# Self-attention of a decoder block: identity cast first, parts stored singly, the maxima's transfers issued by GpSimd, warming matmuls between maxima

## The reference

```python
x = x + _L0_attn_ref(_layernorm(x), Wq, Wk, Wv, Wo)
# in it, with 16 heads of 8 features (dk = 8):
q, k, v = proj(Wq), proj(Wk), proj(Wv)          # [4, 16, 512, 8]
q, k = rotary(q), rotary(k)
scores = q @ k.T / sqrt(8)                       # 512 x 512 for each of 64 heads
out = softmax(scores) @ v
return merge_heads(out) @ Wo.T
```

## Time and profile before

| | us |
|---|---|
| median of 3 executions | 2113.87 |
| fastest, slowest | 2107.86, 2125.06 |
| profiled execution, its own time | 2109.2 |
| its span | 2107.4 |
| first maximum matmul starts | 66.10 |
| first exp starts | 103.65 |
| last exp starts and ends | up to 276.4 |
| output block ends, cross-attention starts | about 308 |

### The profile page before, as it was taken

The page is one execution under the profiler, slowest core; times in us unless marked ns, Lnnn a source line. Parts: engine busy times, 40 slices in busy tenths (PEclk is TensorE's granted clock), DMA queues, the critical chain, the costliest instruction groups (busy, mean ns, idle before and its releaser), DMA issues.

```text
span 2107.4 us, 46811 instructions
## 1 busy us (share of the span) xinstructions
PE 1964.4 (93%) x19020; PEld 1159.9 (55%) x19020; DVE 1525.9 (72%) x1744; ACT 1311.2 (62%) x1857; POOL 995.1 (47%) x722
## 2 busy tenths in 40 slices
PE   6499887779999999999999999999999999999996
PEld 3122133356666666666666666666666666666663
DVE  4599526477877778777877787777877787778762
ACT  3077764456666667666766676666766676667662
POOL 7000004165656555555555565555555565556540
PEclk9599998899999999999999999999999999999998
DMA  4320000044334344333443344533444333343330
GB/s 112 75 54 11 2 32 5 26 121 112 96 101 108 104 127 121 101 99 101 126 113 99 99 111 121 131 93 92 119 121 121 99 89 102 101 117 104 98 104 23
DMA packets 102453, 194.55 MB, mean 92 GB/s; under 512 B 12480, under 2 KB 32448, under 8 KB 102112
## 3 DMA queue, kind: packets, MB, share of 16 engines
q1 hardware_dynamic: 102240, 191.56, 34.6%
HBM read 123.77 MB, written 54.66 MB: 85 GB/s over the span
## 4 chain that ended last, share of the span: by engine, by line
PE 76%; ACT 2%; issue 1%; POOL 1%; DVE 0%; DMA 0%; SPq 0%; ACTq 0%; POOLq 0%
PE ps L1297 16%; PE ps L1372 9%; PE ps L1327 8%; PE ps L1349 8%; PE ps L1382 8%; PE ps L1306 8%; PE ps L1401 6%; PE ps L1360 4%; PE ps L1337 4%; PE ps L1411 3%; PE ps L1322 2%; ACT l_v_tok L1463 1%; PE ps L1389 1%; POOL l_rot L1270 0%; POOL l_rot L1273 0%
## 5 line engine op out<-in xcount | busy, mean ns | idle before, releaser
L1270 POOL TENSOR_TENSOR l_rot<-l_rot,l_rot_s 128x1024 f32<-128x1024 f32 x192 | 455.3, 2371 | 1.0 <-DVE l_rot_s L1614 1.0
L1259 POOL COPY l_kb<-l_kb 128x512 f32<-128x512 f32 x95 | 63.1, 664 | 683.7 <-ACT l_kb L1497 683.7
L1273 POOL TENSOR_TENSOR l_rot<-l_rot,l_norms 128x1024 f32<-128x1024 f32 x192 | 365.2, 1902 | 15.0
L1602 DVE TENSOR_TENSOR l_rot<-ps,l_tab_c 128x1024 f32<-128x1024 f32 x192 | 234.9, 1223 | 164.6 <-ACT l_sq L1471 164.6
L1471 ACT ACTIVATE l_sq<-ps 128x1024 f32<-128x1024 f32 x192 | 196.8, 1025 | 204.5 <-PE ps L1297 201.9
L1614 DVE TENSOR_TENSOR l_rot_s<-ps,l_tab_s 128x512 f32<-128x512 f32 x384 | 245.3, 680 | 0.0
L1593 DVE TENSOR_REDUCE l_norms<-l_sq 128x16 f32<-128x1024 f32 x192 | 232.0, 1208 | 0.0
L1297 PE MATMUL ps<-l_wqkv,xsT 128*128 128x512 f32 x384 | 185.2, 606 | 18.2 <-ACT l_v_tok L1463 15.7
L1497 ACT ACTIVATE l_kb<-ps 64x1024 f32<-64x1024 f32 x192 | 195.7, 1019 | 1.1
L1349 PE MATMUL ps<-l_vb,l_pT 128*32 128x128 f32 x6144 | 188.6, 274 | 2.8 <-ACT l_pT L1463 1.4
L1327 PE MATMUL ps<-l_kb,l_qT 128*32 128x128 f32 x6144 | 187.6, 274 | 0.0
(11 more groups left out here) (172 smaller groups left out, 3170.6 us busy)
## 6 DMA issues: line engine op xcount, KB each, us to landing
l_vb<-v_scratch SPq DMA_DIRECT2D x336, 256.0 KB, 4.5
v_scratch<-l_v_tok SPq DMA_DIRECT2D x96, 512.0 KB, 4.8
l_vb<-v_scratch SPq DMA_DIRECT2D x48, 192.0 KB, 3.1
xsT<-xT SPq DMA_DIRECT2D x48, 135.8 KB, 2.5
stack<-scratch SPq DMA_DIRECT2D x96, 64.0 KB
l_xf<-xT SPq DMA_DIRECT2D x48, 128.0 KB, 2.3
l_wqkv_odd<-wqkv SPq DMA_DIRECT2D x9, 512.0 KB, 6.5
scratch<-parts SPq DMA_DIRECT2D x4, 768.0 KB, 3.7
```

Source lines behind the costliest of these rows:

```text
L1270: nc.gpsimd.tensor_tensor(rot[:, t % 2, n], rot[:, t % 2, n], rot_s[:, n], ALU.add).then_inc(added, 1)
L1273: nc.gpsimd.tensor_tensor(rot[:, t % 2, n], rot[:, t % 2, n], norms[:, t % 2, n, :, None].broadcast_to([P, HEADS, DH]), ALU.mult).then_inc ...
L1602: nc.vector.tensor_tensor(rot[:, t % 2, 1 - r], slot(name, t).rearrange("p n (h d) -> p (n h) d", d=DH), tab_c[:, 1 - r, t % TILES, None, ...
```

## The change

1. GpSimd casts the identity as the first thing after the constants have landed, ahead of its adds; TensorE waits for it only at the first transpose.
2. A batch's three parts are stored by three transfers, each when its part is ready, with a semaphore for each part. All of a batch's stores are issued before its lay-outs, and the lay-outs (the same 24) go part by part. SP does this for all four batches in one run, without the maxima's transfers between them.
3. The maxima's store and loads are issued by GpSimd, behind its last projection step, instead of by SP.
4. `AHEAD` becomes 48. The five warm matmuls stand behind each of the last five pairs of it instead of behind all.
5. A step is now: score, two maximum matmuls, score, score, two maximum matmuls, score, values of the step before, through all batches without a break at a batch's end. Of the two matmuls of a pair the one on rows 64 to 127 comes first.

```diff
@@ -33,8 +33,8 @@
 
 
 
-Q_PARTS = [(0, 3, 0, True), (3, 2, 1, True), (5, 1, 2, True)]
-K_PARTS = [(0, 3, 0, False), (3, 2, 0, False), (5, 1, 0, False)]
+Q_ROWS = [(0, 1, 2), (3, 4), (5,)]
+K_ROWS = [(0, 3, 5), (1, 4), (2,)]
 MAX_ROW = 6 * DK
 
 
...
@@ -102,17 +102,19 @@
         outs = [env["x2T"][:, :, :], env["xsT"][:, :, :].rearrange("p b n -> p (b n)")[:, 0:GROUPS * SEQ]
                 .rearrange("p (g n) -> p g n", g=GROUPS)] + [more_outs[:, b] for b in range(BATCH - 2)]
         probs = sb("probs", [P, RING, SEQ])
+        identb = sb("identb", [P, P], BF16)
+        id_ready = env["sem"]("a_ident_ready")
         with ExitStack() as inner:
 
             project, laid, parts_done = project_parts(env, inner, x, wat, w_attn, consts, cst, scratch, stack, vaug,
-                                                      probs, outs)
-            softmax = softmax_values(env, inner, stack, vaug, probs, outs, max_scratch, laid, parts_done)
+                                                      probs, outs, identb, id_ready)
+            softmax = softmax_values(env, inner, stack, vaug, probs, outs, max_scratch, laid, parts_done, identb,
+                                     id_ready)
 
             with nc.Block() as block:
                 @block.sync
                 def _(sp):
                     project["sync"](sp)
-                    softmax["sync"](sp, project["lay_out"])
 
                 @block.gpsimd
                 def _(pool):
...
@@ -165,11 +168,11 @@
     cosed, sined, rotated = sem("a_cosed"), sem("a_sined"), sem("a_rotated")
     hi_ready, rest_ready, mid_ready = (sem("a_" + n) for n in ("hi", "rest", "mid"))
     lo_ready = [sem(f"a_lo{b}") for b in range(BATCH)]
-    stored = [sem(f"a_stored{b}") for b in range(BATCH)]
+    stored = [sem(f"a_stored{part}") for part in range(3)]
     minus_ones_set = sem("a_minus_ones_set")
     laid_sems = [sem(f"a_laid_out{b}") for b in range(BATCH)]
 
-    laid_count = 16 * (2 + 2 * sum(copies for table in (Q_PARTS, K_PARTS) for _, copies, _, _ in table))
+    laid_count = 16 * (2 + 2 * sum(len(rows) for rows in Q_ROWS + K_ROWS))
     xv = x.rearrange("(t p) d -> p t d", p=P)
 
     STEPS = BATCH + 2
...
@@ -183,11 +186,13 @@
                 sp.dma_start(wat[:, :], w_attn).then_inc(w_ld, 16)
         sp.dma_start(cst[:, CONST["kmask"][0]:], consts[:, CONST["kmask"][0]:]).then_inc(c_ld, 16)
         sp.wait_ge(minus_ones_set, 1)
-        lay_out(sp, 0)
-        lay_out(sp, 1)
+        for b in range(BATCH):
+            store(sp, b)
+            for part in range(3):
+                lay_out(sp, b, part)
         sp.wait_ge(c_ld, 32)
 
-    def lay_out(sp, b):
+    def store(sp, b):
 
         sp.wait_ge(stack_zeroed[b], 1)
         for parity in range(2):
...
@@ -195,17 +200,22 @@
             sp.dma_start(stack[a:a + 2, b, 1, :, :],
                          minus1[:, None, :].broadcast_to([2, PAIRS, SEQ])).then_inc(laid_sems[b], 16)
 
+        sp.wait_ge(hi_ready, b + 1)
+        sp.dma_start(scratch[b, :, 0], parts[:, b % 2, 0]).then_inc(stored[0], 16)
+        sp.wait_ge(mid_ready, b + 1)
+        sp.dma_start(scratch[b, :, 1], parts[:, b % 2, 1]).then_inc(stored[1], 16)
         sp.wait_ge(lo_ready[b], 1)
-        sp.dma_start(scratch[b], parts[:, b % 2]).then_inc(stored[b], 16)
-        sp.wait_ge(stored[b], 16)
-        for qk, table in enumerate((Q_PARTS, K_PARTS)):
+        sp.dma_start(scratch[b, :, 2], parts[:, b % 2, 2]).then_inc(stored[2], 16)
+
+    def lay_out(sp, b, part):
+
+        sp.wait_ge(stored[part], 16 * (b + 1))
+        for qk, rows in enumerate((Q_ROWS, K_ROWS)):
             for parity in range(2):
                 src = scratch[b].rearrange("(c a r) s k t -> a s r k c t", a=2, r=DK)[parity]
-                for row, copies, part, same in table:
-                    for j in range(copies):
-                        a = parity * 64 + (row + j) * DK
-                        sp.dma_start(stack[a:a + DK, b, qk, :, :],
-                                     src[part if same else part + j, :, qk]).then_inc(laid_sems[b], 16)
+                for row in rows[part]:
+                    a = parity * 64 + row * DK
+                    sp.dma_start(stack[a:a + DK, b, qk, :, :], src[part, :, qk]).then_inc(laid_sems[b], 16)
 
     def gpsimd(pool):
         pool.memset(eps, EPS).then_inc(eps_set, 1)
...
@@ -217,6 +227,7 @@
         pool.memset(stack[:, 3], 0.0).then_inc(stack_zeroed[3], 1)
         pool.memset(xT[:, :, 0:PAD], 0.0).then_inc(pads, 1)
         pool.wait_ge(c_ld, 32)
+        nc.gpsimd.tensor_copy(identb[:, :], ident).then_inc(id_ready, 1)
 
         def add(b):
             pool.wait_ge(sined, b + 1)
...
@@ -327,7 +338,8 @@
 
         def high(b):
             if b >= 2:
-                act.wait_ge(stored[b - 2], 16)
+                for part in range(3):
+                    act.wait_ge(stored[part], 16 * (b - 1))
             act.wait_ge(rotated, b + 1)
             nc.scalar.activation(parts[:, b % 2, 0], rc[b % ROTATED], ACT.Copy).then_inc(hi_ready, 1)
 
...
@@ -440,33 +450,29 @@
     for half in reversed(range(HALVES)):
         order.insert((half + 1) * (NM // 2) + 2, (half, "turn"))
     slot_of = {event: n for n, event in enumerate(order)}
-    AHEAD = NM + 20
+    AHEAD = NM + 16
 
     def rows(h):
         return slice(64 * (h % 2), 64 * (h % 2) + 64)
 
-    def sync(sp, lay_out):
+    def gpsimd(pool):
         for half in range(HALVES):
-            if half in (1, 3):
-                lay_out(sp, 2 + half // 2)
             b, h = divmod(half, 2)
-            sp.wait_ge(m_read, slot_of[half, "turn"] + 1)
-            sp.dma_start(max_scratch[half], mrows[:, :]).then_inc(m_stored[half], 16)
-            sp.wait_ge(m_stored[half], 16)
+            pool.wait_ge(m_read, slot_of[half, "turn"] + 1)
+            pool.dma_start(max_scratch[half], mrows[:, :]).then_inc(m_stored[half], 16)
+            pool.wait_ge(m_stored[half], 16)
             for part in range(2):
                 for parity in range(2):
                     a = part * NM + parity * (NM // 2)
                     r = 64 * parity + MAX_ROW + part
-                    sp.dma_start(stack[r:r + 1, b, 0, 4 * h:4 * h + 4, :].rearrange("o c (i q) -> o (c i) q", q=P),
+                    pool.dma_start(stack[r:r + 1, b, 0, 4 * h:4 * h + 4, :].rearrange("o c (i q) -> o (c i) q", q=P),
                                  max_scratch[half, a:a + NM // 2, :].rearrange("(o n) q -> o n q", o=1))\
                         .then_inc(laid[half], 16)
 
     def tensor(pe):
-        pe.wait_ge(id_ready, 1)
-
         def max_scores(half, n):
 
-            b, c, i, parity = half // 2, 4 * (half % 2) + n // 8, n // 2 % TILES, n % 2
+            b, c, i, parity = half // 2, 4 * (half % 2) + n // 8, n // 2 % TILES, 1 - n % 2
             slot = slot_of[half, n // 2]
             if n % 2 == 0 and slot >= 2:
                 pe.wait_ge(m_read, slot - 1)
...
@@ -475,13 +481,15 @@
                 pe.wait_ge(*parts_laid[b])
             m = nc.tensor.matmul(ps[:, 2 * (slot % 2) + parity, :], stack[rows(h), b, 0, c, i * P:(i + 1) * P],
                                  stack[rows(h), b, 1, c, :], start=True, stop=True)
-            if parity:
+            if n % 2:
                 m.then_inc(m_ready, 1)
 
         def turn_max(half):
             slot = slot_of[half, "turn"]
             pe.wait_ge(m_read, slot - 1)
             pe.wait_ge(mlo, half + 1)
+            if half == 0:
+                pe.wait_ge(id_ready, 1)
             nc.tensor.transpose(ps[0:2 * NM, 2 * (slot % 2), 0:P // 2].bitcast(BF16),
                                 mparts[:, :, :], identb[:, :]).then_inc(mt_ready, 1)
 
...
@@ -519,22 +527,23 @@
                 if m % 2 and after < len(order) and order[after][1] == "turn":
                     turn_max(order[after][0])
 
-        stream(0, AHEAD)
-
-
-        for _ in range(WARM_UP):
-            w = nc.tensor.matmul(ps[:, 7, :], ident, env["xT"][:, 0, PAD:], start=True, stop=True)
-        w.then_inc(warm, 1)
-        pe.wait_ge(warm, 1)
-        for b in range(BATCH):
-            for k in range(NU // 4):
-                for j in range(4):
-                    scores(b, 4 * k + j)
-                    m = AHEAD + b * NU + 4 * k + j
-                    stream(m, m + 1)
-                if k >= 1:
-                    values(b, k - 1)
-            values(b, NU // 4 - 1)
+        stream(0, AHEAD - 2 * WARM_UP)
+        for n in range(WARM_UP):
+            m = AHEAD - 2 * (WARM_UP - n)
+            stream(m, m + 2)
+            nc.tensor.matmul(ps[:, 7, :], ident, env["xT"][:, 0, PAD:], start=True, stop=True)
+        for n in range(BATCH * NU // 4):
+            b, k = divmod(n, NU // 4)
+            m = AHEAD + 4 * n
+            scores(b, 4 * k)
+            stream(m, m + 2)
+            scores(b, 4 * k + 1)
+            scores(b, 4 * k + 2)
+            stream(m + 2, m + 4)
+            scores(b, 4 * k + 3)
+            if n >= 1:
```

(31 more changed lines are left out.)

## The result

| | before | changed |
|---|---|---|
| median of 20 executions each, us | 2124.82 | 2107.76 |
| fastest, slowest | 2107.86, 2134.58 | 2098.97, 2120.91 |
| profiled execution, its own time | 2109.2 | 2112.55 |
| its span, mean granted clock | 2107.4, 0.971 | 2110.7, 0.965 |
| first maximum matmul | 66.10 | 60.35 |

The ratio of the medians is 0.9931, with a 95% interval of [0.9911, 0.9952]: 17 us less, where 18 was forecast. The profiled executions show no gain at all: the changed kernel is 8.3 us ahead at the first exp and 2.6 behind at the last. So the agreement of the totals proves nothing, and I went stretch by stretch.

A forecast was written before the change was run, and what follows sets the result against it. The prediction took the late identity cast to hold the start and the order on TensorE to bound the steps. 12.0 + 5.9 + 6.0 - 6 = 18 us less gave 2093 us, range 2081 to 2118.

The forecast's parts named there:

- A: Start of self-attention: cast ahead and part-wise stores start the first maximum matmul at 54.1, 12.0 us less (9 to 13).
- B: Between first maxima and first score: spreading warm matmuls among the last pairs saves 5.9 us (2 to 7).
- C: Attention steps: the new order shortens eight steps from 21.5 to 20.6 us, 6.0 us less (0 to 9).
- D: Maxima's transfers by GpSimd: 1.0 us an issue, late by 0.8 at halves 1 to 6; 6 us lost.
- The tail: End of self-attention: the stall at the last transpose (238.38 to 244.31 for one step) stays.
- Rival 1: Maxima's transfers: GpSimd in time at 0.8 us or less an issue, D nothing, 24 us gained, 2087; chance 0.25.
- Rival 3: Maxima's transfers: GpSimd's issues cost 1.5 us, late by 3.3 at six halves, clock falls, slower at 2120; chance 0.13.
- Rival 4: Start: the cast hid another late thing, lay-outs landing only near 66, A nothing; no chance given.
- rival 2: Attention steps: they do not shorten, C = 0, 12 us gained, 2099; chance 0.17.

The follow-up runs named there:

- kernel 1: The kernel before with only GpSimd's cast of the identity moved ahead: 2113.7 us, ratio 0.9981 to the kernel before.
- kernel 8: The changed kernel without its five warm matmuls: 2102.8 us, ratio 0.9937 to the kernel before.
- kernel 9: The changed kernel with the order of before within a step, the rest unchanged: 2120.0 us in a single execution.
- Kernels 5 and 6: Changed kernel, lay-outs by rows, batches 2 and 3 in four portions between maxima's transfers, these issued by GpSimd (2092.3 us, 0.9897) or SP (2093.8 us, 0.9895).

## Why the prediction was right and wrong

The total was near (17 us against 18, 2107.8 in a range of 2081 to 2118, within 1%), and that was luck: the terms brought less than I counted, and the slow tail, which I had not counted, made up for it. Added to the profiled 2109 or to the first three executions' 2113.9 it gave 2093; the changed kernel's median lies 15 above that, and before's, over twenty executions, is 2124.8. On another chip, the executions side by side, the gain was 13.3 by medians. Step by step:

**A, the start: right in kind, too large.** The cast held the first maximum, as kernel 1 shows, and the part-wise stores let the lay-outs leave at 34.3. The step that failed is "24 x 64 KB = 1,536 KB at about 90 GB/s take 17.1 us", with 12.0 us less: I took the rate as given, though the change reorders those transfers. 1,536 KB at 66 GB/s are 23.3 us, and A brought 5.8. TensorE's start at 60.35 lies outside my bounds of 53 to 57. The part-wise stores and lay-outs were no gain at all: the cast alone brought 9.4 (kernel 1). Why that order is slower is open.

**B, warming between maxima: right, and not cashed.** The last warm matmul ended at 91.59, 31.2 us behind the first maximum, as forecast (97.3 - 66.1 for the first score). The clock rose in the third warm matmul, as worked out. But a score that waits for the maxima doesn't profit: kernel 8 is as fast without them.

**C, the steps: right.** 20.74 for 20.6, shown by kernel 9's 21.49. At 20.74 / 8 = 2.593 a step the term is 50 x 2.695 + 2.39 - 51 x 2.593 = 4.9 us, for 6.0.

**D, GpSimd: the failed step is "an issue costs ... I take 1.0"**, and with it the place of the loss. The issues take 0.49 to 0.55, so a quiet chain is 0.3 from the copy to the issue, 0.55 + 1.43 + 3 x 0.49 and some 1.8 for the last load, 5.6 us, inside the 7.6. By the Trainium skill's figures (DMA: Bandwidth & Descriptors, section Specifications) I had estimated 5.5, and nothing late: the quiet halves agree with it. Time was lost otherwise: the same transfers ran beside SP's bulk transfers, so that scores waited up to 9.2 us at one or two of halves 0 to 2 (3.8 to 14.8 us in all in the eleven traces with GpSimd's transfers and undivided lay-outs). That the sum of the waits was 6.4 us in the first trace, where I had written 6, is chance. I had the row for it, a store that took 7.8 us behind lay-outs, and dismissed it as "used five steps later" while the change shortened just that slack and brought the halves forward onto the lay-outs. At half 0 step A's error came on top: at the lower rate batch 1 was still being laid until about 83 us, not done at 76. The Trainium skill says on the same page, in the section Issuing engines are not separate DMA queues, that transfers started by different engines run on the same 16 DMA engines and interleave. Kernels 5 and 6 agree, in that GpSimd and SP come out alike.

**The tail: missed.** That the stall at the last transpose "stays" was true of TensorE's idling (2.46 us, 1.95 before). What follows was read from one execution: one slow step there, twelve in the next. With the tail kept warm in both, the change is worth 4.8 us side by side (5.8 by means). My terms as measured agree with that: A 5.8, B 5.9 and C 4.9 are 16.6 us, and waits of 6 to 15 us come off. By medians the greater part of the rest is the slow tail, which costs the kernel before 10.6 and 13.3 us and the changed one 2.0 and 2.5 (S of 0, 2 and 10 in its three traces); by means the tail's part is small on one chip. Whether, and why, the clock comes back sooner behind the new steps is open.

**The rivals.** Rival 1, in time, would be 24 us less; portions with the tail warm come near it (19.6 at the last exp). Rival 3 had the wait and the clock's fall right (at halves 0 and 1), but not six times and not by the issue. Rival 4 and rival 2 are excluded by kernels 1 and 9.

## What to carry to other kernels

Keep transfers that are small and awaited from being under way beside bulk ones; here it made no difference whether SP or GpSimd issued them. Fit the bulk into portions between them. When a change brings work forward, look up what else is on the queues at the new time, and don't take a rate over from transfers that the change reorders. Before subtracting from one profile, see in a second which stretches differ between executions of the same program, above all where TensorE has just been idle.

## What was unexpected of the hardware

- In the changed kernel half clock (1.2 GHz) held for ten steps of 3.69 us with TensorE busy 92% of the time (18.49 of 20 us), after 2.46 us idle; in two other executions of the same kernel for two steps and for none. In the kernel before it was one step and twelve.
- The same 24 transfers moved 66 to 91 GB/s at the same 0.57 busy share of the DMA engines, mostly but not only by their order. The cause is open.
- A 16 KB store by GpSimd landed 1.43 us after its issue alone, and up to 11.3 us after it beside SP's 64 KB transfers.
- GpSimd issues a small DMA in 0.49 to 0.55 us (its first in 0.79), SP in 0.28 to 0.54.
